# Moving a block inversion on GpSimd by one pipeline slot, and a dump ahead of its results in the load queue

## The reference

```python
qkvz = hidden_states @ W_qkvz
ba = hidden_states @ W_ba
...
y = jax.nn.silu(y).transpose(0, 2, 1)          # causal convolution of q, k, v over 4 steps
beta = jax.nn.sigmoid(b)
g = -jnp.exp(A_log) * jax.nn.softplus(a + dt_bias)
q = jnp.repeat(_l2norm(q), KV_RATIO, axis=2) * DK ** (-0.5)
k = jnp.repeat(_l2norm(k), KV_RATIO, axis=2)
...
def step(S, inp):
    qt, kt, vt, gt, bt = inp
    S = S * jnp.exp(gt)[:, None, None]
    kv = jnp.einsum('hk,hkv->hv', kt, S)
    delta = (vt - kv) * bt[:, None]
    S = S + kt[:, :, None] * delta[:, None, :]
    o = jnp.einsum('hk,hkv->hv', qt, S)
    return (S, o)
...
gated = core * jax.nn.silu(z)
gated = gated * jax.lax.rsqrt(jnp.mean(gated * gated, axis=-1, keepdims=True) + EPS)
return (gated * norm_w).reshape(B, Tn, VDIM) @ W_out
```

## Time and profile before

| | |
|---|---|
| median of 3 runs | 3036.2 us (3026.6 to 3046.8) |
| profiled execution | 3028.9 us, span 3027.2 us |
| PE busy | 2794.9 us, 92% |
| DVE, ACT, POOL busy | 72%, 60%, 52% |
| mean granted clock of PE in the profiled execution | 0.971 |
| transfers of the 16 DMA engines, share | 18% |

### The profile page before, as it was taken

How to read it: one execution, slowest core, us unless ns; L and a number is a source line. 1 busy time by engine, 2 the same in 40 slices (tenths; PEclk the granted TensorE clock), 3 DMA queues, 4 the chain that set the end, 5 groups by cost and what they waited for, 6 DMA issues and landing times. The chain is left out here.

```text
span 3027.2 us, 75586 instructions
## 1 busy us (share of the span) xinstructions
PE 2794.9 (92%) x24303; PEld 1909.6 (63%) x24303; DVE 2181.0 (72%) x4677; ACT 1812.3 (60%) x6310; POOL 1565.5 (52%) x3737
## 2 busy tenths in 40 slices
PE   5999489999999999999999999999999999869998
PEld 4556256666666666666666666666666666655555
DVE  3443468878877887877778778877788788547676
ACT  3321557777766776777677667766677677332332
POOL 1000456667666666666667666766666666410000
PEclk9999789999999999999999999999999999979999
DMA  3000132212222222212122212122222222110000
GB/s 88 1 1 0 28 59 40 45 38 45 42 48 43 49 43 44 49 35 49 35 49 42 54 37 51 39 46 38 45 40 52 42 49 42 24 42 1 8 7 15
DMA packets 485567, 113.74 MB, mean 38 GB/s; under 512 B 423296, under 2 KB 484336, under 8 KB 485168
## 3 DMA queue, kind: packets, MB, share of 16 engines
q1 hardware_dynamic: 485168, 108.76, 18.0%
HBM read 80.63 MB, written 28.06 MB: 36 GB/s over the span
## 5 line engine op out<-in xcount | busy, mean ns | idle before, releaser
L1216 DVE SCALAR_TENSOR_TENSOR S<-S,gs,bank 128x128 f32<-128x128 f32 x1024 | 287.3, 343 | 232.3 <-PE bank L776 228.0
L1247 DVE SCALAR_TENSOR_TENSOR conv<-raw,ckq,conv 128x512 f32<-128x512 f32 x384 | 302.2, 799 | 110.4 <-ACT conv L1001 104.1
L539 POOL TENSOR_TENSOR btmp<-Bk,Tb 64x14 f32<-64x14 f32 (+6 forms) x896 | 339.7, 379 | 66.1 <-POOL Tb L543 0.9
L543 POOL TENSOR_TENSOR Tb<-Tb,btmp 64x14 f32<-64x14 f32 (+6 forms) x896 | 315.2, 352 | 70.9 <-POOL btmp L539 1.3
L986 ACT ACTIVATE sq_gat<-gat 128x128 bf16<-128x128 f32 x512 | 151.8, 297 | 279.2 <-DVE gat L1232 279.2
L1247 DVE SCALAR_TENSOR_TENSOR conv<-raw,cv,conv 128x512 f32<-128x512 f32 x384 | 291.6, 772 | 12.2 <-ACT conv L1001 7.3
L528 POOL TENSOR_TENSOR Tb<-Bk,lower 64x256 f32<-64x256 f32 x64 | 56.0, 875 | 434.8 <-issue 429.0
L1020 ACT ACTIVATE gatn<-gat,ty 128x128 f32<-128x128 f32 x512 | 163.5, 390 | 181.3 <-POOL ty L518 181.3
L733 PE MATMUL bank<-xnT,wkq 128*128 128x512 f32 x512 | 255.8, 623 | 11.6 <-POOL mkX L425 10.7
L749 PE MATMUL bank<-wz_h,xnT 128*128 128x256 f32 x1024 | 260.6, 401 | 0.0
L819 PE MATMUL bank<-wout_h,gT 128*128 128x256 f32 x1024 | 257.0, 394 | 0.0
(11 more groups left out here) (354 smaller groups left out, 6660.1 us busy)
## 6 DMA issues: line engine op xcount, KB each, us to landing
rowb<-decay_rows SPq DMA_DIRECT2D x256, 64.0 KB, 3.9
blk_n<-N SPq DMA_DIRECT2D x256, 64.0 KB, 2.5
Tp<-blk_t SPq DMA_DIRECT2D x128, 128.0 KB, 2.9
Wp<-blk_w SPq DMA_DIRECT2D x128, 128.0 KB, 3.0
wkq<-in_L_attn_W_qkvz_dram SPq DMA_DIRECT2D x32, 128.0 KB, 2.3
wv<-in_L_attn_W_qkvz_dram SPq DMA_DIRECT2D x16, 256.0 KB, 3.6
Bk<-blk_n SPq DMA_DIRECT2D x64, 64.0 KB, 2.6
blk_t<-Tb SPq DMA_DIRECT2D x64, 64.0 KB, 2.5
```

What stands on the lines that cost most here:

```text
L539: pool.tensor_tensor(tmp, Bk[:, j, j + 1:].unsqueeze(2).broadcast_to([64, 15 - j, j]), Tb[:, j, 0:j].unsqueeze(1).broadcast_to([64, 15 - j ...
L543: pool.tensor_tensor(Tb[:, j + 1:, 0:j], Tb[:, j + 1:, 0:j], tmp, ALU.subtract).then_inc(row_rdy, 1)
L1216: i = dve.scalar_tensor_tensor(out=S[:, 2 * b + v, :], in0=S[:, 2 * b + v, :], scalar=gs[t.c][:, kind, 2 * h + v:2 * h + v + 1], in1=pKU[b ...
L1247: dve.scalar_tensor_tensor(out=y, in0=raw[h][:, j, :, :, k:k + H].rearrange("p c b n -> p (c b) n"), scalar=cw[:, j, k:k + 1], in1=y, op0= ...
```

## The change

`base_first` moves from lag `S_F` to lag `S_F + 1`, and `base_rest` and `base_out`, which are written as lag 4, to `S_F + 3`, which is 5. So the first part of the inversion is done in the even slot n + 1, behind `causal`, and the second part in the odd slot n + 2; `x16` stays in slot n + 3. In SP's slot `dump` now stands ahead of `base_out`. `base_start` also takes the values that it waits for into registers beforehand, which changes no wait.

```diff
 def base_out(s):
-    t = s.back(4)
+    t = s.back(S_F + 3)
     if not t.live or t.c % 2:
         return
...
 def body(s):
     base_load(s)
     weights(s)
     out_weights(s)
     decays(s)
     value_weights(s)
+    dump(s)
     base_out(s)
-    dump(s)
...
 def base_first(s):
-    t = s.back(S_F)
+    t = s.back(S_F + 1)
     if not t.live or t.c % 2 == 0:
         return
     base_start(t)
...
 def base_rest(s):
-    t = s.back(4)
+    t = s.back(S_F + 3)
     if not t.live or t.c % 2:
         return
```

More of the change, by code:

```diff
@@ L520, in base_start @@
                 def base_start(t):
-                    read, sent = held(pool, t.pairs(16, 16)), held(pool, t.pairs(16))
+                    read, sent, begun, ones = (held(pool, v) for v in (
+                        t.pairs(16, 16), t.pairs(16), t.pairs(2, 1), t.pairs(2, 2)))
                     pool.wait_ge(m["made"], 2)
@@ L529, in base_start @@
                     pool.wait_ge(m["made"], 2)
-                    pool.wait_ge(base_in, t.pairs(2, 1))
+                    pool.wait_ge(base_in, begun)
                     pool.memset(Tb[:].rearrange("p i c -> p (i c)")[:, ::17], 1.0).then_inc(base_in, 1)
-                    pool.wait_ge(base_in, t.pairs(2, 2))
+                    pool.wait_ge(base_in, ones)
                 def base_row(t, j):
```

## The result

The changed kernel takes 3330.8 us (median of 4 runs, 3329.3 to 3344.0) against 3031.4 us for the kernel before in the same comparison: a ratio of 1.0997, 95% interval 1.0933 to 1.1061. It is 10% slower. The forecast was 3315 us.

A forecast was written before the change was run, and what follows sets the result against it. PE was taken to bound the kernel, at least 33.80 us a pair. 3029 us, plus 235 for x16's wait and the low clock, plus 48 for head loads, gave 3312; predicted 3315 us, range 3180 to 3430.

The forecast's parts named there:

- PE bound, pair of 33.80 us at the least: PE works 16.90 us a slot without idle time, so an even and odd slot together take at least 33.80 us.
- The first part's move frees the 2.03 us: GpSimd's late out_scale and PE's idle time before solve in even slots go: at most 2.03 us a pair.
- Tb is complete 16.40 us into the odd slot: On GpSimd, causal ends at 8.41 us, the nine last rows take 7.99, so Tb is ready at 16.40.
- x16 waits 3.7 us: In each even slot PE stands 3.7 us before x16 for the Tp loads; bounds 3.4 and 4.8.
- the term "2.56": On SP's load queue, the first read into Tp is issued 2.56 us after the write of Tb, when that has landed.
- The clock costs 2.0 us a pair: After the wait before x16, PE runs partly at the lower clock: 2.0 us a pair, ends 0.2 and 2.8.
- The head loads cost 3.2 us, 15 times: In a head's first slot PE waits 3.2 us more before the projection for wkq and ckq: 48 us in all.
- 64 pairs: The extra 3.67 us a pair (39.5 against 35.83) was counted for all 64 pairs: 235 us.
- The share of PE, 84 to 85%: Sign in the profile after: PE's busy share of the span falls to 84 to 85%.
- The clock holding: Rival: the wait before x16 is there but PE's clock does not fall; 3197 us, chance 13%.
- The faster rival: Tb ready by 12.7 us into the odd slot, x16 never waits, 2899 us; change pays from 14.7 down; chance 3%.
- the queue's part: Dump of N ahead of base_out on SP's queue: N reaches DRAM in time, Bk lands at 8.4 us, hidden.

The follow-up runs named there:

- a_split10_heads: Changed kernel with inversion rows 1 to 10 in the even slot, 11 to 14 in the odd, and next head's wkq and ckq loads ahead of base_out: 2939.0 us, ratio 0.9735.
- a_split7: Changed kernel with elimination rows 6 and 7 moved back into the first part (rows 1 to 7, then 8 to 14): 3219.5 us, ratio 1.0666.
- a_split9: Changed kernel with elimination rows 6 to 9 moved back into the first part (rows 1 to 9, then 10 to 14): 3080.7 us, ratio 1.0219.
- a_filler17: Changed kernel with 17 unread 128x128 matmuls put ahead of x16's wait in each even slot: 3220.7 us, ratio 1.0669.
- a_filler26: Changed kernel with 26 unread 128x128 matmuls put ahead of x16's wait in each even slot: 3294.0 us, ratio 1.0919.

## Why the prediction was right, point by point

*PE bound, pair of 33.80 us at the least.* Right as far as the runs go: the odd slots stayed at 16.89, and the shortest pairs, those of a_split10_heads, have 34.55 us in the mean (17.15 + 17.40).

*The first part's move frees the 2.03 us.* Right: no wait before `solve` in the stretch; GpSimd's wait for Bk fell from 6.7 us a pair to 0.8.

*Tb is complete 16.40 us into the odd slot.* Right: 16.36, with the nine rows begun at 8.37 (the prediction named a start before 8.4 as a sign of being wrong, and 0.03 us is none). The reading of GpSimd's slot as a fixed offset from PE's held. That cover was the matter is shown by a_split7 and a_split9, where x16's wait follows the rows moved.

*x16 waits 3.7 us.* Right mechanism, too small: 4.35 in the mean. In the usual pair it is 3.9, of which 0.2 is the second read: it lands after 3.1 us in the median, and the 2.9 of the forecast is the median of first and second reads together. The rest is pairs in which the write of Tb lands late. From the write to the read it is over 2.7 us in 22 of the 58 pairs, up to 4.3, and 2.97 in the mean: the term "2.56" was read from one pair, and should have been taken from the spread of landing times.

*The clock costs 2.0 us a pair.* 2.13 in the slots without a head's loads, 3.0 in the heads' first; a_filler17 gives the 2.1 back by keeping PE busy.

*The head loads cost 3.2 us, 15 times.* Too large: 26 us in all, 1.7 each. The last ckq load was issued 9.0 us into the even slot of 1400.49, near the forecast's 8.3, but PE came to the projection later, being held at x16 for 5.5 us and then at the low clock, so the same delay was hidden once more.

*64 pairs.* The sum took the steady pair's cost 64 times; it applies to the 58 of the stretch, 5.12 us each against 4.42 forecast (3.67 and the heads' share). The six pairs outside it cost 5 us together: they wait 28 us for Tp as well, but before the change PE stood 34 us there for conv (L711), and now it is 18 us (L712), so that much of the new wait seems to stand in the place of an old one. Too many pairs and too much for the heads' loads go against too short a wait. That 283 us of forecast and 302 measured lie as close as they do is in part luck.

*The share of PE, 84 to 85%.* Wrong: 87%. The sum left out that matmuls at the lower clock are busy for longer, 101 us in all.

*The rivals.* The clock holding is refuted by the windows at 0.85 and by a_filler17. The faster rival's first threshold, 12.7 us for no wait at all, is borne out by a_split10_heads. Its second, that the change pays from 14.7 us on down, is not: in a_split9 Tb is ready at 13.69 in every odd slot, and the kernel is still 2.2% slower. There x16 waits 1.5 us in the mean of the slots without a head's loads, 1.0 by the prediction's terms; the clock takes 0.4 more, and the heads still wait for ckq. The prediction has the queue's part only as a repair of the change's own harm; alone it is worth 1.9%, which stands in no term of the sum.

## What to carry to other kernels

When a step is moved in a software pipeline, count the time from its last instruction through every write, read and landing to its first reader, at the reader's place inside its slot; here that was 6.2 us against 2.5 us of room, and the fine position within the slot decided, not the number of slots. A long step may be split at any row: at the row where both neighbours still have slack, the move that cost 10% as a whole slot came to a small gain, 0.8% over the reordered queue alone. And the order in a shared load queue is not neutral merely because nobody waits for the moved transfer: here it changed when the others were issued and how soon they landed.

## What the runs showed of the hardware that was not expected

The same write takes 2.5 us to land in most pairs and up to 4.2 in others. In the changed kernel the write of Tb landed after 2.5 us in the pair from 1318.49 and after 4.1 in the one from 1358.66. The DMA view of the two stretches between write and read (busy share of the 16 DMA engines in 40 equal slices, in tenths; queue: packets, MB, share; then KB and us to landing):

```profile
DMA  0000000000000000000026988888794000002688
...
blk_t<-Tb SPq DMA_DIRECT2D x1, 64.0 KB, 2.5
```

```profile
DMA  0000000080003877784000499989410010000000
...
q8 instruction: 1, 0.02, 2.2%
...
blk_t<-Tb SPq DMA_DIRECT2D x1, 64.0 KB, 4.1
```

In the slow one a transfer of 16 KB of the instruction queue (q8) stands beside the write, in the fast one none does. The 58 writes of the stretch bear this out: 36 landed after 2.46 to 2.49 us and two after 2.8 and 3.0, all without such a transfer between issue and landing; the 20 that took 3.1 to 4.2 us all had one. It is not enough by itself: in the kernel before, 16 of the 44 quick writes had one too, but nearly all of these came 2.0 us or later after the write's issue. This is what the traces show side by side; no run moves these transfers, so the cause was not tested.

One of a_filler26's matmuls of 128x128 (fp32) took 0.23 us of PE's time (6.0 us for 26; the profile counts each as two instructions, 225 − 173 = 52 in the slot), where a transpose of `front_tp`, which it counts as one, takes 0.13 (four start at 1359.13 and the next group 0.53 later). And filling a wait with useless matmuls made the kernel 3% faster (a_filler17), the clearest sign here of what the clock is worth.
